# The chain in front of the state-space loop, by halves, and the first state's input made by VectorE

## The chip, the cores and the metric

One core of a Trainium2 chip runs the whole program. The metric is the device time of one launch in microseconds (us), the median of three runs. A 128 x 128 TensorE multiplies, VectorE (DVE) and ScalarE (ACT) work from SBUF and from PSUM, where TensorE writes, GpSimd (POOL) works from SBUF alone, and SyncE (SP) issues the DMAs. All five run their own instruction streams and wait for one another on semaphores.

## The reference, cut to what matters

Four sequences of 512 tokens with 128 features pass six layers: tree-routed feed-forward, attention, tree-routed feed-forward, mixture of experts, state-space block, mixture of experts. The change touches the state-space block:

```python
xz = rmsnorm(residual) @ W_in                     # 128 -> 2 x 256
x, z = split(xz)
x = silu(causal_conv4(x) + conv_b)
x_dbl = x @ W_x                                   # 64 + 16 + 16 columns
dt = softplus(x_dbl[:, :64] @ W_dt + b_dt)        # 256 channels
B, C = x_dbl[:, 64:80], x_dbl[:, 80:96]
# for each of 16 states n, over 512 tokens t:
#   h[t] = exp(dt[t] * A[:, n]) * h[t-1] + dt[t] * x[t] * B[t, n]
#   y[t] += h[t] * C[t, n]
out = residual + ((y + x * D) * silu(z)) @ W_out
```

softplus(v) is worked out as max(v, 0) + log(1 + u) with u = exp(-|v|); for small u the logarithm is corrected: with c = (1 + u) - 1, the result is max(v, 0) + u + min(max(log(1 + u) - c, -u*u/2), 0).

## The kernel before

Channels or tokens lie on the 128 partitions. The 24 units of work (6 layers, 2 sequences side by side, 2 pairs) run one after another; a unit's norm and transposes are done inside the unit before it, by `hand_over`, at fixed steps of its loop. Four units are state-space units, of which each does the following for one sequence, with its 256 channels as two halves m = 0, 1 of 128 partitions by 512 tokens.

**The front**, in the order of the chain. TensorE forms `W_in` products; ACT and DVE the convolution and silu, which give `n_xc`. TensorE multiplies by `W_x` (L1754): rows 0 to 63 of bank 4 are the input of dt, rows 64 to 95 are B and C. ACT copies the dt rows (L1003). TensorE makes B once more with tokens on partitions (L1758, 16 small matmuls to bank 5) and then the dt product of both halves (L1763, banks 0 and 1). ACT takes |v| for each half (L1006), then for both halves together u = exp(-|v|) (L1008), log(1 + u) (L1010), u*u/2 (L1011), and max(v, 0) by halves (L1013). DVE makes c (L1402), the difference (L1404), the two bounds and + u (L1406, L1407) over both halves at once, then dt (L1410) and dt*x (L1413) by halves. TensorE turns dt*x so that tokens lie on partitions (`dtx_rows`, L1461, banks 4 and 5).

**The loop** has 16 states with two halves each, numbered i = 0 to 31. ACT multiplies the turned dt*x by B per token (`inputs`, L1038, 4 instructions a state, tile `n_sx`) and makes exp(dt*A) (`decays`, L1030, tile `n_da`); TensorE turns the product back into PSUM (`drive(i)`, banks 0, 1 and 6 in turn, L1461); DVE scans (L1419, tile `n_h`); POOL multiplies by C (L791, `n_hc`), and TensorE adds that up with an identity matmul (L1784). C has to stand on all partitions, so SP writes its 16 rows to DRAM and reads them back broadcast, two states a DMA, into the ring `n_cs` of three (`state_rows`, L588 and L594). `n_sx[:, 0]` and `n_sx[:, 1]` also hold max(v, 0) and the correction ahead of the loop, `n_da` the logarithm and the square, and `n_h` |v| and u.

The order on each engine is the order of the code. DVE's `step` makes the instruction behind it wait until the one in it is done.

## Time and profile before

| | |
|---|---|
| median of 3 runs | 1404.59 us (1404.09 to 1405.96) |
| the profiled execution's own time | 1403.94 us |
| its span, first to last instruction | 1402.2 us |
| outside its span | 1.74 us |
| mean granted TensorE clock | 0.953 of 2.4 GHz |
| busy: PE, DVE, ACT, POOL | 1225.4, 916.9, 650.7, 237.3 us |
| state-space units | 4 of 24; first scans at 480.8, 565.0, 1169.3 and 1253.6 us |

Busy times overlap across engines, and a busy PE is not PE at its peak. In rows of the timeline the first number is the start in the span, the second the duration (of all merged instructions where there is a count over 1), and a bracket gives the idle time of the engine just before and what ended it.

### The profile page before, as it was taken

What the parts mean: (1) busy time and instruction counts of PE and PEld (TensorE: products, weight loads), DVE (VectorE), ACT (ScalarE), POOL (GpSimd) and SP (SyncE); (2) the same over time, 40 slices, a digit from 0 to 9 for tenths busy, and PEclk for the clock granted to TensorE, in tenths of its full rate; (3) what the DMA queues carried; (4) which work ended last, traced back from release to release, by engine and by line L of the source; (5) the groups of instructions that cost most, each with busy time, mean ns of one, the idle gap of its engine ahead of it and who ended that gap; (6) DMA issues with size and microseconds to landing.
All of it is one profiled execution on the core that took longest, in us unless ns stands there. A gap on an engine that the chain in (4) does not pass through costs nothing.

```text
span 1402.2 us, 17312 instructions
## 1 busy us (share of the span) xinstructions
PE 1225.4 (87%) x6135; PEld 798.9 (57%) x6184; DVE 916.9 (65%) x1802; ACT 650.7 (46%) x1199; POOL 237.3 (17%) x207
## 2 busy tenths in 40 slices
PE   5998788999899686889999967889999995969898
PEld 3676344577666343546667743446766653545565
DVE  6766766455567595877764766655555858859665
ACT  4543445443322785942234434453442247679122
POOL 3000000000020271741000010000002004718110
PEclk9999899999999798899999999999999996979999
DMA  6203020000110111120200122100010101112120
GB/s 216 61 23 105 25 69 19 2 0 1 61 60 1 58 64 46 61 76 1 69 23 0 38 69 78 33 2 1 1 40 21 61 22 55 46 46 76 61 68 8
DMA packets 31941, 62.02 MB, mean 44 GB/s; under 512 B 4112, under 2 KB 19760, under 8 KB 31664
## 3 DMA queue, kind: packets, MB, share of 16 engines
q1 hardware_dynamic: 31856, 60.93, 13.7%
q8 instruction: 49, 0.80, 0.2%
q14 instruction: 36, 0.29, 0.1%
HBM read 53.11 MB, written 8.32 MB: 44 GB/s over the span
## 4 chain that ended last, share of the span: by engine, by line
PE 66%; DVE 16%; ACT 8%; issue 3%; DMA 3%; POOL 2%; SPq 1%; another core or an unknown queue 0%; DVEq 0%; ACTq 0%; POOLq 0%
PE bank L1452 12%; PE bank L1454 12%; PE bank L1453 12%; PE bank L1618 8%; PE bank L1461 5%; DVE a_mx L1366 3%; DVE n_h L1419 3%; ACT n_sx L1038 3%; PE bank L1530 2%; PE bank L1784 2%; PE bank L1677 2%; PE bank L1591 2%; ACT n_da L1030 2%; DMA a_k<-stack_dram 2%; POOL n_hc L791 1%
## 5 line engine op out<-in xcount | busy, mean ns | idle before, releaser
L1215 DVE SCALAR_TENSOR_TENSOR f_hl<-bank,f_hh 128x512 fp32r<-128x512 f32 x192 | 131.8, 689 | 128.2 <-ACT f_hh L867 127.3
L867 ACT ACTIVATE f_hh<-bank 128x512 fp32r<-128x512 f32 x192 | 114.6, 597 | 188.2 <-PE bank L1530 150.0
L929 ACT ACTIVATE m_sl<-bank 128x512 f32<-128x512 f32 x144 | 85.8, 597 | 220.8 <-PE bank L1454 220.3
L791 POOL TENSOR_TENSOR n_hc<-n_h,n_cs 128x512 f32<-128x512 f32 x128 | 159.9, 1276 | 141.5 <-DVE n_h L1419 140.3
L1452 PE MATMUL bank<-xT_h,mw_h 128*128 128x512 f32 x288 | 160.8, 558 | 7.0 <-DVEq L514 4.3
L1419 DVE TENSOR_TENSOR_SCAN n_h<-n_da,bank 128x512 f32<-128x512 f32 x128 | 149.1, 1206 | 21.4 <-PE bank L1461 18.1
L1618 PE MATMUL bank<-m_h,mw 128*128 128x512 f32 x288 | 145.6, 594 | 0.0
L1366 DVE TENSOR_REDUCE a_mx<-bank 128x1 f32<-128x384 f32 (+3 forms) x176 | 106.1, 637 | 51.9 <-PE bank L1717 49.6
L1282 DVE TENSOR_TENSOR m_t<-m_sl,bank 128x512 f32<-128x512 f32 x128 | 87.9, 687 | 73.5 <-PE bank L1454 72.2
L1784 PE MATMUL bank<-n_hc,ident 128*128 128x512 f32 x256 | 132.4, 607 | 1.3 <-POOL n_hc L791 1.3
L947 ACT ACTIVATE a_p<-bank 128x1024 f32<-128x1024 f32 (+3 forms) x128 | 87.8, 703 | 91.1 <-PE bank L1654 90.0
L722 POOL TENSOR_TENSOR small<-small,half 128x4 f32<-128x4 f32 x24 | 24.3, 1011 | 597.1 <-DVE small L1117 596.7
L1461 PEld LDWEIGHTS bank<-ident,n_sx 128*128 128x128 f32 x512 | 67.3, 154 | 91.0 <-issue 68.0
L1454 PE MATMUL bank<-xT_h,mw_l 128*128 128x512 f32 x288 | 115.1, 400 | 0.0
L1452 PE MATMUL bank<-f_hh,fw_h 128*128 128x512 f32 x192 | 109.4, 570 | 6.1 <-DVE f_hl L1215 6.1
L1453 PE MATMUL bank<-xT_l,mw_h 128*128 128x512 f32 x288 | 114.6, 398 | 0.0
L1038 ACT ACTIVATE n_sx<-bank,n_bT 128x256 f32<-128x256 f32 x256 | 103.0, 536 | 9.7 <-PE bank L1461 9.7
L1461 PE MATMUL bank<-ident,n_sx 128*128 128x128 f32 x512 | 85.1, 299 | 25.4 <-DVE n_h L1419 14.5
L1030 ACT ACTIVATE n_da<-n_dt,amat 128x512 f32<-128x512 f32 x128 | 91.1, 794 | 17.7 <-DVE n_h L1419 12.9
L1715 PE MATMUL bank<-a_k,a_q 128*128 128x128 bf16 (+3 forms) x246 | 67.5, 317 | 29.5 <-DVE a_mx L1366 17.7
L1452 PE MATMUL bank<-xT_h,fw_h 128*128 128x512 f32 x192 | 83.2, 433 | 0.9 <-POOL b1w L705 0.9
L1290 DVE TENSOR_TENSOR m_h<-m_t,m_c 128x512 f32<-128x512 f32 x112 | 77.6, 693 | 4.4 <-DMA m_c<-comb_dram 0.7
(232 smaller groups left out, 2358.5 us busy)
## 6 DMA issues: line engine op xcount, KB each, us to landing
n_cs<-c_dram SPq DMA_DIRECT2D x32, 512.0 KB, 3.7
m_c<-comb_dram SPq DMA_DIRECT2D x28, 512.0 KB, 5.2
a_q<-stack_dram SPq DMA_DIRECT2D x8, 512.0 KB, 4.3
a_k<-stack_dram SPq DMA_DIRECT2D x16, 256.0 KB, 5.2
stage_fw<-in_fw_dram SPq DMA_DIRECT2D x6, 512.0 KB, 6.8
...
```

The costliest lines, as they stand in the source:

```text
L791: n_hcs.by(nc.gpsimd.tensor_tensor(n_hc[:, i % 4, :], n_h[:, i % 4, :], n_cs[:, j % C_RING, i // 2 % 2, :], ALU.mult))
L1030: n_das.by(act.activation(n_da[:, i % 4, :], n_dt[:, i % 2, :], ACT.Exp, scale=amat[:, i % 2, i // 2:i // 2 + 1]))
L1038: ins = act.activation(n_sx[:, n % 2, c, :], dtx_rows(c), ACT.Copy, scale=n_bT[:, c, n:n + 1])
L1215: f_lo.by(V.scalar_tensor_tensor(f_h[1][:, i % 4, :], bank[:, i % 3, :], 0.0, f_h[0][:, i % 4, :].bitcast(F32), ALU.max, ALU.subtract))
L1366: a_m1.by(V.tensor_reduce(a_mx[:, quad, qt, h0:h0 + nh], src, AX_X, ALU.max, negate=True))
L1419: n_scan.by(V.tensor_tensor_scan(n_h[:, i % 4, :], n_da[:, i % 4, :], drive(i), 0.0, ALU.mult, ALU.add))
L1452: mm(dst, w[0], x[0], start=start, stop=False)
L1453: mm(dst, w[0], x[1], start=False, stop=False)
L1454: return mm(dst, w[1], x[0], start=False, stop=stop)
L1461: ins = nc.tensor.transpose(dst(t), src(t), idn)
L1618: m_s2.by(mm(bank[:, 6, :], mw2[:, e, m, :], m_h[:, i2 % 3, :], start=i2 == 0, stop=i2 == MSTEPS - 1))
L1784: n_ya.by(mm(bank[:, 2 + m, :], ident[:], n_hc[:, i % 4, :], start=n == 2, stop=n == NSTATE + 1))
```

## The change

The dt product of both halves is put before the 16 matmuls of B on TensorE. max(v, 0) passes from ACT to DVE. The logarithm and the square are taken by halves, alternating; DVE adds u to max(v, 0) early, and the difference, the bounds, dt and dt*x go through for half 0 and then for half 1. dt is now one instruction that takes the last bound and adds. For state 0, DVE multiplies dt*x by B itself and writes the product straight to `drive(0)` and `drive(1)` in PSUM; the B row comes broadcast from DRAM (`n_brow`, in the third slot of the C ring), so the DMA to DRAM carries 32 rows in place of 16, and the third C load waits until that row has been read. ACT's `inputs(0)` and the eight transposes of state 0 are gone.

```diff
+        n_brow = n_cs[:, 2, 0, :]
...
-                n_cwr.by(sp.dma_start(c_dram, n_crow[80:96]))
+                n_cwr.by(sp.dma_start(c_dram, n_crow[64:96]))
                 sp.wait_ge(n_cwr.sem, n_cwr.at(k, 0))
+                n_b0.by(sp.dma_start(n_brow, c_dram[0:1].to_broadcast([P, T])))
                 for j in range(C_LOADS):
+                    if j == 2:
+
+                        sp.wait_ge(n_db0.sem, n_db0.at(k, 1))
...
-                n_lns.by(act.activation(n_ln, n_u, ACT.Ln, bias=1.0))
-                n_sqs.by(act.activation(n_sq, n_u, ACT.Square, scale=HALF_ROOT))
                 for m in range(2):
-                    n_poss.by(act.activation(n_pos[:, m, :], bank[:, m, :], ACT.Relu, bias=b_dt[:, m:m + 1]))
+                    n_lns.by(act.activation(n_ln[:, m], n_u[:, m], ACT.Ln, bias=1.0))
+                    n_sqs.by(act.activation(n_sq[:, m], n_u[:, m], ACT.Square, scale=HALF_ROOT))
...
-                inputs(k, 0)
...
+                for m in range(2):
+                    dve.wait_ge(n_abss.sem, n_abss.at(k, m))
+                    n_poss.by(V.tensor_scalar(n_pos[:, m], bank[:, m, :], b_dt[:, m:m + 1], 0.0, ALU.add, ALU.max))
                 dve.wait_ge(n_btp.sem, n_btp.at(k, 0))
                 n_bts.by(V.tensor_copy(flat(n_bT[:]), bank[:, 5, 0:NT * NSTATE]))
...
+                step(V.tensor_scalar(n_cor, n_u, 1.0, -1.0, ALU.add, ALU.add))
+                step(V.tensor_tensor(n_pos, n_pos, n_u, ALU.add))
...
+                for m in range(2):
+                    dve.wait_ge(n_lns.sem, n_lns.at(k, m))
+                    step(V.tensor_tensor(n_cor[:, m], n_ln[:, m], n_cor[:, m], ALU.subtract))
+                    dve.wait_ge(n_sqs.sem, n_sqs.at(k, m))
+                    step(V.scalar_tensor_tensor(n_cor[:, m], n_sq[:, m], -1.0, n_cor[:, m], ALU.mult, ALU.max))
+                    n_dts.by(V.scalar_tensor_tensor(n_dt[:, m], n_cor[:, m], 0.0, n_pos[:, m], ALU.min, ALU.add))
                     dve.wait_ge(n_dts.sem, n_dts.at(k, m))
                     n_dtxs.by(V.tensor_tensor(n_dtx[:, m], n_dt[:, m], n_xc[:, m], ALU.mult))
+                dve.wait_ge(n_b0.sem, n_b0.at(k, 0))
+                for m in range(2):
+                    dve.wait_ge(n_dtxs.sem, n_dtxs.at(k, m))
+                    n_db0.by(V.tensor_tensor(drive(m), n_dtx[:, m], n_brow, ALU.mult))
...
-                    if n < NSTATE:
-                        pe.wait_ge(n_sxs.sem, n_sxs.at(k, n))
+                    if 1 <= n < NSTATE:
+                        pe.wait_ge(n_sxs.sem, n_sxs.at(k, n - 1))
```

On DVE, in the first state-space unit, between the copy of B and C out of PSUM and the first two scans (a scan is printed as SCALAR_TENSOR_TENSOR here), the order before is this; `n_sx` is the correction and `n_xp` is dt*x:

```order
L1395 COPY n_hc<-bank 32x512
L1397 COPY n_bT<-bank 128x64
L1402 TENSOR_SCALAR n_sx<-n_h 128x1024
L1404 TENSOR_TENSOR n_sx<-n_da,n_sx 128x1024
L1406 SCALAR_TENSOR_TENSOR n_sx<-n_da,n_sx 128x1024
L1407 SCALAR_TENSOR_TENSOR n_sx<-n_sx,n_h 128x1024
L1410 TENSOR_TENSOR n_dt<-n_sx 128x512 x2
L1413 TENSOR_TENSOR n_xp<-n_dt,n_xc 128x512 x2
L1419 SCALAR_TENSOR_TENSOR n_h<-n_da,bank 128x512 x2
```

The order of the change, from the instruction that makes c on, after the two max(v, 0) (L1403) and the copy of B (L1405):

```order
L1409 TENSOR_SCALAR n_sx<-n_h 128x1024
L1410 TENSOR_TENSOR n_sx<-n_sx,n_h 128x1024
L1414 TENSOR_TENSOR n_sx<-n_da,n_sx 128x512
L1416 SCALAR_TENSOR_TENSOR n_sx<-n_da,n_sx 128x512
L1417 SCALAR_TENSOR_TENSOR n_dt<-n_sx 128x512
L1419 TENSOR_TENSOR n_xp<-n_dt,n_xc 128x512
L1414 TENSOR_TENSOR n_sx<-n_da,n_sx 128x512
L1416 SCALAR_TENSOR_TENSOR n_sx<-n_da,n_sx 128x512
L1417 SCALAR_TENSOR_TENSOR n_dt<-n_sx 128x512
L1419 TENSOR_TENSOR n_xp<-n_dt,n_xc 128x512
L1423 TENSOR_TENSOR bank<-n_xp,n_cs 128x512 x2
L1432 SCALAR_TENSOR_TENSOR n_h<-n_da,bank 128x512 x2
```

Four instructions over 1024 elements became two over 1024 and eight over 512, and two products that write PSUM (L1423) now stand straight before the scans.

On ACT the same place runs from the table load of the logarithm to the second state's decays; before:

```order
L1010 ACT_TABLE_LOAD
L1010 ACTIVATE n_da<-n_h 128x1024
L1011 ACTIVATE n_da<-n_h 128x1024
L1013 ACTIVATE n_sx<-bank,col 128x512 x2
L1030 ACT_TABLE_LOAD
L1030 ACTIVATE n_da<-n_dt,amat 128x512 x2
L1038 ACTIVATE n_sx<-bank,n_bT 128x256 x8
```

and in the change:

```order
L1018 ACT_TABLE_LOAD
L1018 ACTIVATE n_da<-n_h 128x512
L1019 ACTIVATE n_da<-n_h 128x512
L1018 ACTIVATE n_da<-n_h 128x512
L1019 ACTIVATE n_da<-n_h 128x512
L1035 ACT_TABLE_LOAD
L1035 ACTIVATE n_da<-n_dt,amat 128x512 x2
L1043 ACTIVATE n_sx<-bank,n_bT 128x256 x4
```

The number of table loads is the same, max(v, 0) is gone from ACT, and four `n_sx` instructions stand in place of eight.

On TensorE, from the `W_x` product on; before:

```order
L1754 MATMUL bank<-n_xc,wx 96x512 x2
L1758 MATMUL bank<-wx,n_xc 128x16 x8
L1763 MATMUL bank<-n_hc,wdt 128x512 x2
L1461 MATMUL bank<-ident,n_xp 128x128 x8
L1461 MATMUL bank<-ident,n_sx 128x128 x20
L1784 MATMUL bank<-n_hc,ident 128x512
```

and in the change:

```order
L1767 MATMUL bank<-n_xc,wx 96x512 x2
L1771 MATMUL bank<-n_hc,wdt 128x512 x2
L1774 MATMUL bank<-wx,n_xc 128x16 x8
L1474 MATMUL bank<-ident,n_xp 128x128 x8
L1474 MATMUL bank<-ident,n_sx 128x128 x12
L1796 MATMUL bank<-n_hc,ident 128x512
```

The dt product (L1763, now L1771) stands ahead of the B matmuls, and 12 transposes of `n_sx` in place of 20 come before the first addition of a state to y.

## Rows read from the trace of the kernel before

**Rows 1.** Timeline of the first unit's front: matmuls and ACT

```profile
461.98 1.85 PE L1758 MATMUL bank<-wx,n_xc 128*128 128x16 f32 x16
462.42 0.57 ACT L1003 ACTIVATE n_hc<-bank 64x512 f32<-64x512 f32 x1
...
463.77 2.10 PE L1763 MATMUL bank<-n_hc,wdt 64*128 64x512 f32 x4
...
466.62 1.06 ACT L1008 ACTIVATE n_h<-n_h 128x1024 f32<-128x1024 f32 x1
467.69 1.28 ACT L1010 ACT_TABLE_LOAD   x1
```

**Rows 2.** Timeline of the first unit's front: logarithm to loop

```profile
467.71 0.69 DVE L1402 TENSOR_SCALAR n_sx<-n_h 128x1024 f32<-128x1024 f32 x1 [3.61 <-ACT n_h L1008]
468.99 1.06 ACT L1010 ACTIVATE n_da<-n_h 128x1024 f32<-128x1024 f32 x1
469.95 1.04 ACT L1011 ACTIVATE n_da<-n_h 128x1024 f32<-128x1024 f32 x1
470.14 1.23 DVE L1404 TENSOR_TENSOR n_sx<-n_da,n_sx 128x1024 f32<-128x1024 f32 x1 [1.74 <-ACT n_da L1010]
...
472.16 1.28 ACT L1030 ACT_TABLE_LOAD   x1
...
473.92 1.29 DVE L1410 TENSOR_TENSOR n_dt<-n_sx 128x512 f32<-128x512 f32 x2
474.65 1.33 ACT L1030 ACTIVATE n_da<-n_dt,amat 128x512 f32<-128x512 f32 x2 [1.20 <-DVE n_dt L1410]
475.13 1.28 DVE L1413 TENSOR_TENSOR n_xp<-n_dt,n_xc 128x512 f32<-128x512 f32 x2
...
475.96 1.94 PE L1461 MATMUL bank<-ident,n_xp 128*128 128x128 f32 x8 [10.10 <-DVE n_xp L1413]
477.94 3.02 ACT L1038 ACTIVATE n_sx<-bank,n_bT 128x256 f32<-128x256 f32 x8 [1.96 <-PE bank L1461]
...
479.65 3.35 PE L1461 MATMUL bank<-ident,n_sx 128*128 128x128 f32 x16 [1.75 <-ACT n_sx L1038]
480.77 2.33 DVE L1419 TENSOR_TENSOR_SCAN n_h<-n_da,bank 128x512 f32<-128x512 f32 x2 [4.36 <-PE bank L1461]
480.80 1.38 ACT L1030 ACTIVATE n_da<-n_dt,amat 128x512 f32<-128x512 f32 x2
482.03 1.61 ACT L1038 ACTIVATE n_sx<-bank,n_bT 128x256 f32<-128x256 f32 x4
```

**Rows 3.** Timeline of DVE: third scan here, first scans of the last unit

```profile
484.52 4.54 DVE L1419 TENSOR_TENSOR_SCAN n_h<-n_da,bank 128x512 f32<-128x512 f32 x4
...
1253.60 2.33 DVE L1419 TENSOR_TENSOR_SCAN n_h<-n_da,bank 128x512 f32<-128x512 f32 x2 [4.36 <-PE bank L1461]
```

**Rows 4.** Timeline of ACT in the loop: its waits, units one and two

```profile
495.45 0.72 ACT L1030 ACTIVATE n_da<-n_dt,amat 128x512 f32<-128x512 f32 x1 [3.73 <-DVE n_h L1419]
...
576.95 0.72 ACT L1030 ACTIVATE n_da<-n_dt,amat 128x512 f32<-128x512 f32 x1 [0.97 <-DVE n_h L1419]
578.06 0.73 ACT L1030 ACTIVATE n_da<-n_dt,amat 128x512 f32<-128x512 f32 x1 [0.39 <-DVE n_h L1419]
```

**Rows 5.** Durations of one line: times min/median/max in ns, then form

```profile
L996 ACT ACTIVATE n_xc<-n_hc x4: 629/630/630, 458.0 to 1231.4; 128x512 f32<-128x512 f32 x4
L1397 DVE COPY n_bT<-bank x4: 224/224/225, 463.9 to 1236.8; 128x64 f32<-128x64 f32 x4
L1383 DVE TENSOR_SCALAR n_hc<-n_xp,col x4: 545/546/548, 455.1 to 1228.5; 128x512 f32<-128x512 f32 x4
```

**Rows 6.** Timeline of SP: the C loads of the first unit

```profile
464.55 24.10 SPq L594 DMA_DIRECT2D n_cs<-c_dram  x4
```

**Rows 7.** Windows: busy by engine, granted clock, DMA share, GB/s

```profile
470.00:472.00 2.00, 0.00 (x0) 0.00 (x0) 1.82 (x2) 2.00 (x4) 0.00 (x0) 0.50 0.15 61
482.00:484.00 2.00, 1.31 (x10) 1.00 (x9) 1.97 (x6) 2.00 (x6) 1.93 (x2) 0.86 0.00 0
```

More of the change, by code:

```diff
@@ L469, in program @@
         n_us = sig("n_us", "mamba", 1)
-        n_lns = sig("n_lns", "mamba", 1)
-        n_sqs = sig("n_sqs", "mamba", 1)
+        n_lns = sig("n_lns", "mamba", 2)
+        n_sqs = sig("n_sqs", "mamba", 2)
         n_poss = sig("n_poss", "mamba", 2)
+        n_b0 = sig("n_b0", "mamba", 1, 16)
+        n_db0 = sig("n_db0", "mamba", 2)
         n_dts = sig("n_dts", "mamba", 2)
@@ L475, in program @@
         n_dxt = sig("n_dxt", "mamba", 1)
-        n_sxs = sig("n_sxs", "mamba", NSTATE)
+        n_sxs = sig("n_sxs", "mamba", NSTATE - 1)
         n_das = sig("n_das", "mamba", 2 * NSTATE)
-        n_dbs = sig("n_dbs", "mamba", 2 * NSTATE)
+        n_dbs = sig("n_dbs", "mamba", 2 * NSTATE - 2)
         n_scan = sig("n_scan", "mamba", 2 * NSTATE)
@@ L1033, in inputs @@
             def inputs(k, n):
-                if n >= 2:
-                    act.wait_ge(n_dbs.sem, n_dbs.at(k, 2 * n - 3))
+                if n >= 3:
+                    act.wait_ge(n_dbs.sem, n_dbs.at(k, 2 * n - 5))
                 for c in range(NT):
@@ L1400, in mamba @@
                 dve.wait_ge(n_us.sem, n_us.at(k, 0))
+                dve.wait_ge(n_poss.sem, n_poss.at(k, 1))
+                step(V.tensor_scalar(n_cor, n_u, 1.0, -1.0, ALU.add, ALU.add))
+                step(V.tensor_tensor(n_pos, n_pos, n_u, ALU.add))
                 dve.wait_ge(n_sil.sem, n_sil.at(k, 3))
-                step(V.tensor_scalar(n_cor, n_u, 1.0, -1.0, ALU.add, ALU.add))
-                dve.wait_ge(n_lns.sem, n_lns.at(k, 0))
-                step(V.tensor_tensor(n_cor, n_ln, n_cor, ALU.subtract))
-                dve.wait_ge(n_sqs.sem, n_sqs.at(k, 0))
-                step(V.scalar_tensor_tensor(n_cor, n_sq, -1.0, n_cor, ALU.mult, ALU.max))
-                step(V.scalar_tensor_tensor(n_cor, n_cor, 0.0, n_u, ALU.min, ALU.add))
-                for m in range(NHALF):
-                    dve.wait_ge(n_poss.sem, n_poss.at(k, m))
-                    n_dts.by(V.tensor_tensor(n_dt[:, m], n_cor[:, m], n_pos[:, m], ALU.add))
-                for m in range(NHALF):
+                for m in range(2):
[4 more added lines that the diff above has]
+                    n_dts.by(V.scalar_tensor_tensor(n_dt[:, m], n_cor[:, m], 0.0, n_pos[:, m], ALU.min, ALU.add))
                     dve.wait_ge(n_dts.sem, n_dts.at(k, m))
                     n_dtxs.by(V.tensor_tensor(n_dtx[:, m], n_dt[:, m], n_xc[:, m], ALU.mult))
+                dve.wait_ge(n_b0.sem, n_b0.at(k, 0))
+                for m in range(2):
+                    dve.wait_ge(n_dtxs.sem, n_dtxs.at(k, m))
+                    n_db0.by(V.tensor_tensor(drive(m), n_dtx[:, m], n_brow, ALU.mult))
                 for i in range(2 * NSTATE):
-                    dve.wait_ge(n_dbs.sem, n_dbs.at(k, i))
+                    if i < 2:
+                        dve.wait_ge(n_db0.sem, n_db0.at(k, i))
+                    else:
+                        dve.wait_ge(n_dbs.sem, n_dbs.at(k, i - 2))
                     dve.wait_ge(n_das.sem, n_das.at(k, i))
@@ L1755, in mamba @@
                 n_xdb.by(ins)
+                pe.wait_ge(n_dtc.sem, n_dtc.at(k, 0))
+                for m in range(2):
+                    n_dtp.by(mm(bank[:, m, :], wdt[:, m, :], n_dtr, start=True, stop=True))
                 for c in range(NT):
@@ L1760, in mamba @@
                 n_btp.by(ins)
-                pe.wait_ge(n_dtc.sem, n_dtc.at(k, 0))
-                for m in range(2):
-                    n_dtp.by(mm(bank[:, m, :], wdt[:, m, :], n_dtr, start=True, stop=True))
                 pe.wait_ge(n_bts.sem, n_bts.at(k, 0))
```

4 lines of the change are left out of this document (2 added, 2 removed).

## The prediction

> **What bounds the kernel now.** The page comes first: TensorE is the busiest engine, but that is a mean over 24 units, and the change lies in four stretches of some 18 us each, the fronts of the state-space units. So I read the timeline there. From the dt product to the first scan it shows one thread that passes from engine to engine, never two of them busy with what the end waits for. TensorE multiplies B for 1.85 us and then dt; ACT has had the input of dt ready since 462.42 + 0.57 = 462.99, but the dt product starts at 463.77, because the B matmuls stand ahead of it [rows 1]. Then u ends at 467.68, a table load and the logarithm end at 470.05, and only there does DVE begin three instructions of 1.22 to 1.23 us over both halves, two for dt and two for dt*x [rows 2]. TensorE idles 10.10 us, turns dt*x in 1.94 us, ACT multiplies by B, TensorE turns back, and DVE, which was done at 476.41, scans at 480.77 after 4.36 us of idleness [rows 2]. All four units repeat this: the last unit's first scan waits the same 4.36 us [rows 3].
>
> Whether time won there reaches the end is read from the loop. After two scans and some 1.4 us of statistics DVE scans again at 484.52 [rows 3]; through the middle of the loop the timeline shows it busy without a gap, while ACT waits for scans: 3.73 us in the first unit, 0.97 and 0.39 us in the second [rows 4]. So DVE's start sets the loop up to there. From there to the end ACT and TensorE share the bound, and both hang on that same moment. A loop that starts d earlier thus ends d earlier, as long as ACT isn't left behind by more than those waits.
>
> **The change part by part**, with the first unit's times. Dependent DVE instructions start their duration plus 0.03 us apart (three from 470.14 to 473.92, 1.26 each [rows 2]), independent ones of 512 elements 0.61 us apart (two in 1.29, each of them 0.68 to 0.69).
>
> *dt before B.* The dt product can start 0.06 us after 462.99, so at 463.05 in place of 463.77. Everything on ACT up to u comes 0.72 us earlier; u ends at 466.96. The B matmuls move behind it: 463.05 + 2.10 + 1.85 = 467.00, then DVE's copy of 0.22 us [rows 5] ends at 467.29. It was hidden before; now it stands before the instruction that makes c, and costs that 0.3 us.
>
> *Early part on DVE.* c takes 0.69 us as before [rows 2], 467.32 to 468.01; max(v, 0) + u costs like a two-source instruction over 1024, 1.23 us, and ends at 469.27. It is 1.23 us moved to where DVE used to wait for the logarithm (1.74 us of idleness). The two max(v, 0) on DVE lie between |v| and u, where DVE had nothing (3.61 us idle). Their duration isn't in the trace for this form; between 0.55 (512 elements from SBUF, [rows 5]) and 0.75 they are done by 466.7, so the price is nil.
>
> *Logarithm by halves.* Table load of 1.28 us, then 0.63 us for 512 elements on ACT [rows 5], 0.10 less from start to start: 468.27 to 468.90 for the first logarithm, the last square done by 470.5. DVE is ready at 469.30, so ACT no longer sets the pace; 0.4 us of its lead is unused. No table load is added.
>
> *The chain by halves.* Half 0: difference, bound, dt at 0.72 us each (0.69 for 512 elements) from 469.30, dt*x at 471.46. Half 1 starts 0.61 us later at 472.07, and its dt*x runs 474.23 to 474.91. The last dt*x ended at 476.41 before, so 1.5 us are won. ACT's table load for the exponential ends at 471.8, decays run at once behind dt of each half, and the second is done by 474.9, before any scan needs it.
>
> *State 0 by DVE.* Two products of 512 elements. No DVE instruction of this trace writes PSUM; the bounds are 0.55 us (the fastest of 512 elements [rows 5]) and 1.17 us (half of two scans in 2.33 [rows 2]). I take 0.69, what two SBUF sources cost here, since the arithmetic is the same. Starts at 474.84 and 475.44, first scan at 476.05. Before: 480.77. **Won: 4.72 us.** The way over TensorE and ACT (1.94 + 1.5 + 1.1 us) is no longer in front of the scans.
>
> *What is late next.* dt*x of half 1 is done at 474.91, its four transposes take half of 1.94 us, so ACT starts `inputs(1)` at 475.97, 1.61 us long; it is ready for state 1's decays at 477.4 against 480.80, a lead of 3.4 us [rows 2]. State 1 is turned from 477.6 on in 1.1 us (479.65 to 480.77 before), ready at 478.7; the third scan wants it at 484.52 - 4.72 = 479.80. State 2 follows: ACT 478.6 to 480.2, turned by 481.35, wanted at 482.1. The first scans are fed. ACT's lead is 1.3 us short of DVE's, which the waits of 3.73 us, and of 0.97 + 0.39 = 1.36 us in the second unit, just take up [rows 4].
>
> *DMAs.* SP issues its loads from 464.55, when the write to DRAM has landed [rows 6]. Three loads of 512 KB were through early in the 470 to 472 window (share 0.15 [rows 7]). Now the 256 KB of the B row go first and two loads behind: at most five sixths of that, so before 470.3, and the row is wanted at 474.84. The write has 32 rows in place of 16; it lies between the end of the `W_x` product, near 462, and 464.55, so twice as long would cost the row 2.5 us at most of its 4.5 us of margin. The third load leaves at 476.1 with nothing behind it but loads that wait for POOL anyway; POOL wants it from the ninth scan, after 489.
>
> *TensorE's clock.* It stands at 0.50 through the front and is back at full speed in the window 482 to 484 (0.86, [rows 7]), some 3 us after the transposes of 479.65 began. In the new order the fifth state-half's transposes and the first addition to y fall at 480.3 to 483. At 1.2 GHz that addition takes an estimated 1.5 to 2 us (two of the four dt instructions of 2.10 us at full speed, doubled at most), and the sixth scan slips by 0.6 to 0.9 us; at 2.4 GHz it doesn't. I take 0.2 us. The Trainium skill says ("TensorE: Matmul & The Clock Gate", What's actually happening) that the clock is half by default and sustained activity releases it; the trace agrees, 0.50 and then 0.86. By that rule TensorE, which now has eight transposes fewer and more pauses between short bursts, would come back later, if at all earlier; that is a rival below.
>
> *Sum.* 4.72 - 0.2 = 4.5 us a unit, 18.0 us in four. The profiled execution took 1403.94 us (span 1402.2 and 1.74 around it); 1403.94 - 18.0 = 1385.9. The median is 0.65 us above that execution, so 1386.6 us.
>
> **The rivals.**
>
> *The loop keeps ACT's lead only.* If ACT or TensorE binds in the first states, the gain is ACT's 3.4 us a unit: 1404.6 - 13.6 = 1391.0. For it: ACT has no gap for the first 10 us of the loop, and the second unit's slack exceeds the need by 0.06 us. Against it: the waits of [rows 4].
>
> *The clock comes back late.* Then the sixth scan slips 0.9 us, and further transposes with it, say 2 us a unit: 1404.6 - 4 x 2.7 = 1393.8. The clock decides from how soon dense work begins, which is 2 us earlier than before.
>
> *The time is already covered, or the B row is late.* If the row landed at 479.6 the first scan would stand where it stood: 1404.6. Against it the margin of 4.5 us.
>
> *Slower.* TensorE falls to 1.2 GHz within the last 15 us of the loop, where it binds. There a state-half takes TensorE an estimated 1.3 us at full speed: half of the dt product's 2.10 us [rows 1], and four transposes, which take a quarter of 1.94 us at 2.4 GHz [rows 2], less some overlap. At half speed that is about 1.3 us more, and with four such state-halves a unit 5.2 us are lost against 4.7 won: 1404.6 + 4 x 0.5 = 1406.6, and from 3.6 state-halves on it decides. For it: the clock also falls inside the loop in some units, after pauses. Against it: in that stretch TensorE has no pauses.
>
> **How the numbers follow.** Forecast 0.64 (1384 to 1389), ACT's lead 0.14, late clock 0.10, covered 0.04, slower 0.04, and 0.04 for more than forecast. The low end: PSUM writes of 0.55 us and no slip give 5.0 us, 1384.6; with 0.1 us less on each of the four shared steps 1383. The high end: PSUM writes of 1.17 us cost 0.96 more and the sixth scan 0.6, leaving 3.2 us, 1392; with the late clock 1393.8. Range 1383 to 1393.5. A measurement of this kernel can tell about 0.2% (2.8 us) from no change: faster than that 0.91, within it 0.05, slower 0.04.
>
> **What would show it.** In the changed profile: the dt product starts right after ACT's copy; DVE's chain from the first difference to the first scan is 6.7 us without a gap; two DVE products into `bank` of about 0.69 us each; the first scans without idle time before them; from first scan to the end of each loop 51.6 us as before or 0.2 more. It is wrong if that last distance grows by 1 us or more (ACT or the clock), if those products take over a microsecond, or if DVE waits on the DMA of the B row.

## The result, and the profile after

The change takes 1390.65 us (median of 4 runs, 1390.03 to 1391.93) against 1404.34 us for the kernel before (4 runs, 1402.42 to 1405.96) in the same comparison: ratio 0.9904, 95% interval 0.9887 to 0.9921. It is 13.7 us faster, where 18.0 were forecast. The profiled span is 1388.2 us in place of 1402.2.

The page after: busy time, share of the span and instructions of each engine, and TensorE's granted clock in 40 slices.

```profile
PE 1234.8 (89%) x6152; PEld 800.1 (58%) x6152; DVE 927.7 (67%) x1826; ACT 641.8 (46%) x1183; POOL 237.6 (17%) x207
...
PEclk9999899999999798899999999999999996979899
```

TensorE is busy for 9.4 us more, with 32 transposes fewer: some of its work ran at a lower clock. To see where, each unit is cut in two at places that stand in both programs. The **front** runs from the start of DVE's copy of B and C (L1395, now L1400) to the first scan, the **loop** from there to the first `n_da<-n_xc,col,bank` on DVE (L1428, now L1441).

| us, units 1 to 4 | fronts | loops | sum |
|---|---|---|---|
| before | 18.52, 18.47, 18.41, 18.48 | 51.60, 51.51, 51.59, 51.52 | 280.10 |
| after | 14.37, 13.67, 14.76, 14.28 | 52.10, 52.19, 52.29, 52.34 | 266.00 |
| won | 4.15, 4.80, 3.65, 4.20 | -0.50, -0.68, -0.70, -0.82 | 14.1 |

The fronts won 16.8 us, the loops lost 2.7, and the difference of 14.1 is the result within 0.4 us.

**The front** of unit 1, timeline of the changed kernel; this answers to [rows 1, 2]:

```profile
462.16 0.57 ACT L1010 ACTIVATE n_hc<-bank 64x512 f32<-64x512 f32 x1
462.79 1.98 PE L1771 MATMUL bank<-n_hc,wdt 64*128 64x512 f32 x4 [0.90 <-ACT n_hc L1010]
...
464.70 2.74 PE L1774 MATMUL bank<-wx,n_xc 128*128 128x16 f32 x16
...
465.53 1.06 ACT L1015 ACTIVATE n_h<-n_h 128x1024 f32<-128x1024 f32 x1
...
467.48 0.22 DVE L1405 COPY n_bT<-bank 128x64 f32<-128x64 f32 x1 [1.20 <-PE bank L1774]
467.62 0.68 DVE L1409 TENSOR_SCALAR n_sx<-n_h 128x1024 f32<-128x1024 f32 x1
...
469.60 0.69 DVE L1414 TENSOR_TENSOR n_sx<-n_da,n_sx 128x512 f32<-128x512 f32 x1
...
474.56 0.69 DVE L1419 TENSOR_TENSOR n_xp<-n_dt,n_xc 128x512 f32<-128x512 f32 x1
...
475.17 1.29 DVE L1423 TENSOR_TENSOR bank<-n_xp,n_cs 128x512 f32<-128x512 f32 x2
...
476.37 2.32 DVE L1432 TENSOR_TENSOR_SCAN n_h<-n_da,bank 128x512 f32<-128x512 f32 x2
```

The dt product starts 0.06 us behind ACT's copy, the first scan has no bracket, and from the first difference to the scan DVE takes 476.37 - 469.60 = 6.77 us without a gap. One row is off: u is ready at 465.53 + 1.06 = 466.59, yet c (L1409) starts at 467.62, because DVE's copy of B stands ahead of it and waits for TensorE. The B matmuls took 2.74 us where 1.85 had been measured [rows 1]. In the four units they take 2.74, 1.96, 3.13 and 2.58 us, and the fronts follow: 14.37, 13.67, 14.76 and 14.28.

**The loop.** TensorE and DVE in its first 10 us, timeline after:

```profile
478.17 1.94 PE L1474 MATMUL bank<-ident,n_sx 128*128 128x128 f32 x8 [1.75 <-ACT n_sx L1043]
...
480.10 3.43 DVE L1432 TENSOR_TENSOR_SCAN n_h<-n_da,bank 128x512 f32<-128x512 f32 x3
...
481.66 1.91 PE L1796 MATMUL bank<-n_hc,ident 128*128 128x512 f32 x2
...
483.37 1.06 PE L1474 MATMUL bank<-ident,n_sx 128*128 128x128 f32 x4
...
484.47 1.22 DVE L1432 TENSOR_TENSOR_SCAN n_h<-n_da,bank 128x512 f32<-128x512 f32 x1 [0.93 <-PE bank L1474]
```

The first addition to y takes 1.91 us, the transposes behind it 1.06, and the sixth scan waits 0.93 us for them. It does so in all four units, at 8.10 us from the first scan. The clock over that stretch, windows after (columns as in [rows 7]):

```profile
466.00:468.00 2.00, 1.44 (x7) 1.33 (x7) 0.80 (x3) 1.97 (x3) 0.00 (x0) 0.50 0.46 168
...
482.00:484.00 2.00, 2.00 (x5) 0.86 (x4) 1.53 (x2) 2.00 (x6) 2.00 (x3) 0.50 0.00 0
484.00:486.00 2.00, 2.00 (x6) 0.86 (x5) 1.47 (x4) 2.00 (x6) 1.11 (x1) 0.50 0.52 172
486.00:488.00 2.00, 2.00 (x12) 1.44 (x11) 1.93 (x5) 1.30 (x4) 1.27 (x1) 0.96 0.28 90
```

The clock is at 0.50, 1.2 GHz, until 486, nearly 10 us into the loop. In the other units it comes back 8 to 10 us into it. Before, the loop's first scan was at 480.77 and the full clock back some 2 us later: 0.86 in 482 to 484 [rows 7].

### The profile page after: what moved, and what is told of

Read it like the earlier page. It is cut to its first block, busy times and chain, and to the rows that moved or that the text cites. A ratio compares the mean times of both kernels' runs of the same rounds, so it can differ in the third digit from the quotient of the medians.

```text
span 1388.2 us, 17313 instructions
## 1 busy us (share of the span) xinstructions
PE 1234.8 (89%) x6152; PEld 800.1 (58%) x6152; DVE 927.7 (67%) x1826; ACT 641.8 (46%) x1183; POOL 237.6 (17%) x207
## 3 DMA queue, kind: packets, MB, share of 16 engines
q1 hardware_dynamic: 32496, 62.11, 14.1%
## 4 chain that ended last, share of the span: by engine, by line
PE 69%; DVE 16%; ACT 6%; issue 3%; DMA 3%; POOL 2%; SPq 2%; DVEq 0%; ACTq 0%; POOLq 0%
PE bank L1465 12%; PE bank L1466 12%; PE bank L1467 12%; PE bank L1631 9%; PE bank L1474 6%; PE bank L1796 4%; DVE a_mx L1371 3%; PE bank L1543 3%; PE bank L1604 2%; PE bank L1690 2%; ACT n_sx L1043 2%; DVE n_h L1432 2%; PE bank L1665 1%; DMA a_k<-stack_dram 1%; PE bank L1728 1%
## 5 line engine op out<-in xcount | busy, mean ns | idle before, releaser
L1796 PE MATMUL bank<-n_hc,ident 128*128 128x512 f32 x256 | 136.9, 625 | 1.5 <-POOL n_hc L798 1.5
L1474 PEld LDWEIGHTS bank<-ident,n_sx 128*128 128x128 f32 x480 | 63.6, 154 | 83.5 <-issue 61.8
L1728 PE MATMUL bank<-a_k,a_q 128*128 128x128 bf16 (+3 forms) x256 | 72.4, 324 | 32.3 <-DVE a_mx L1371 20.4
L1043 ACT ACTIVATE n_sx<-bank,n_bT 128x256 f32<-128x256 f32 x240 | 97.5, 541 | 7.1 <-PE bank L1474 7.1
L1474 PE MATMUL bank<-ident,n_sx 128*128 128x128 f32 x480 | 81.2, 299 | 17.0 <-ACT n_sx L1043 10.8
L1465 PEld LDWEIGHTS bank<-xT_h,mw_h 128*128 128x128 f32 x288 | 55.6, 193 | 43.5 <-issue 27.8
```

The source lines that it names most:

```text
L1043: ins = act.activation(n_sx[:, n % 2, c, :], dtx_rows(c), ACT.Copy, scale=n_bT[:, c, n:n + 1])
L1465: mm(dst, w[0], x[0], start=start, stop=False)
L1474: ins = nc.tensor.transpose(dst(t), src(t), idn)
L1796: n_ya.by(mm(bank[:, 2 + m, :], ident[:], n_hc[:, i % 4, :], start=n == 2, stop=n == NSTATE + 1))
```

## The experiments

The theory after this reading: (F) the fronts are as forecast, but for the copy of B, which waits for matmuls at half clock; (L) the loops are longer because TensorE is at half clock for the first 8 to 10 us of them. The scans say where: in the change the seventh scan starts 0.47 to 0.67 us later after the first than before, in every unit, and unit 4 loses another 0.35 between the 12th and the 15th; hardly anything is lost elsewhere. The rivals: ACT's lead is what limits the gain (it gives the measured 1391 too), and the halves, not state 0, carry the gain or the loss.

All edits are against the changed kernel, e11 against the one before. The kernels before had medians of 1404.7 (e1 to e4), 1405.3 (e5 to e8), 1407.0 (e9 to e11) and 1405.7 us (e12), and runs of one kernel scattered by some 0.3%, so the fronts and loops of the profiles say more than the medians:

| | median us | ratio (95%) | fronts | loops | sum |
|---|---|---|---|---|---|
| the change | 1390.65 | 0.9904 (0.9887 to 0.9921) | 13.7 to 14.8 | 52.1 to 52.3 | 266.0 |
| e1 B first | 1390.99 | 0.9905 (0.9881 to 0.9930) | 14.2 | 52.1 to 52.2 | 265.4 |
| e2 copy late | 1386.86 | 0.9868 (0.9843 to 0.9892) | 13.5 to 13.6 | 52.0 to 52.1 | 262.6 |
| e3 y late | 1394.38 | 0.9926 (0.9904 to 0.9948) | 13.6 to 14.9 | 52.1 to 52.9 | 267.4 |
| e4 warm | 1385.99 | 0.9864 (0.9840 to 0.9887) | 13.6 to 14.5 | 51.6 to 51.9 | 262.7 |
| e5 state 0 by ACT | 1400.02 | 0.9955 (0.9937 to 0.9974) | 16.6 to 17.7 | 51.5 to 51.6 | 274.9 |
| e6 whole | 1388.89 | 0.9879 (0.9855 to 0.9903) | 13.2 to 14.2 | 52.5 to 52.9 | 265.7 |
| e7 copy late, y late | 1388.78 | 0.9874 (0.9849 to 0.9898) | 13.5 to 13.6 | 52.0 to 52.4 | 262.8 |
| e8 whole, copy late, warm | 1388.12 | 0.9870 (0.9847 to 0.9894) | 13.2 to 13.3 | 51.7 to 52.5 | 261.4 |
| e9 copy late, warm | 1385.78 | 0.9845 (0.9826 to 0.9863) | 13.5 to 13.6 | 52.0 to 52.8 | 263.8 |
| e10 as e8, fewer extras | 1385.97 | 0.9845 (0.9825 to 0.9866) | 13.2 to 13.3 | 51.5 to 52.3 | 260.5 |
| e11 before, only state 0 by DVE | 1398.98 | 0.9941 (0.9924 to 0.9959) | 15.2 | 52.4 to 52.7 | 271.0 |
| e12 as e9, warmed earlier | 1388.04 | 0.9871 (0.9852 to 0.9891) | 13.5 to 13.6 | 51.5 to 52.8 | 261.8 |

### The copy of B: e1 and e2

e1 puts the B matmuls back ahead of the dt product. e2 keeps dt first and moves DVE's copy of B behind max(v, 0) + u:

```diff
-                pe.wait_ge(n_dtc.sem, n_dtc.at(k, 0))
-                for m in range(2):
-                    n_dtp.by(mm(bank[:, m, :], wdt[:, m, :], n_dtr, start=True, stop=True))
                 ... the 16 matmuls of B
+                pe.wait_ge(n_dtc.sem, n_dtc.at(k, 0))
+                for m in range(2):
+                    n_dtp.by(mm(bank[:, m, :], wdt[:, m, :], n_dtr, start=True, stop=True))
```

> The changed kernel with the 16 B matmuls put back ahead of the dt product. My theory (the B matmuls behind dt run into TensorE's fall to 1.2 GHz and hold the copy of B, and with it DVE): u comes 0.72 us later, but the copy of B is out of the way, so from the copy of B and C to the first scan all four units take 14.2 us, against 14.37, 13.67, 14.76 and 14.28 in the changed kernel; total within 0.5 us of it. Rival (moving dt ahead is worth its 0.72 us a unit): 2.9 us slower than the changed kernel, that is 1393.5 us.

```diff
-                dve.wait_ge(n_btp.sem, n_btp.at(k, 0))
-                n_bts.by(V.tensor_copy(flat(n_bT[:]), bank[:, 5, 0:NT * NSTATE]))
...
                 step(V.tensor_tensor(n_pos, n_pos, n_u, ALU.add))
+                dve.wait_ge(n_btp.sem, n_btp.at(k, 0))
+                n_bts.by(V.tensor_copy(flat(n_bT[:]), bank[:, 5, 0:NT * NSTATE]))
```

> The changed kernel with DVE's copy of B behind the addition of u to max(v, 0). My theory: c starts 0.03 us after u, and the first scan comes 13.6 us after the copy of B and C in all units, 0.05 to 1.1 us earlier than now, 2.6 us over four units: 1388.0 us. Rival (the front is not what sets the loop's end, ACT's lead is): no change, 1390.6 us.

e1: fronts of 14.15 to 14.23, in sum 0.3 us less than the change's, as its text expected: with the copy where it stood, dt first had won nothing. e2: fronts of 13.51 to 13.58, all four alike, with DVE in unit 1 as follows (timeline of e2):

```profile
466.83 0.69 DVE L1407 TENSOR_SCALAR n_sx<-n_h 128x1024 f32<-128x1024 f32 x1 [0.34 <-ACT n_h L1015]
467.55 1.23 DVE L1408 TENSOR_TENSOR n_sx<-n_sx,n_h 128x1024 f32<-128x1024 f32 x1
468.81 0.23 DVE L1410 COPY n_bT<-bank 128x64 f32<-128x64 f32 x1
...
475.72 2.32 DVE L1432 TENSOR_TENSOR_SCAN n_h<-n_da,bank 128x512 f32<-128x512 f32 x2
```

c now waits for u from ACT and the copy for nobody. The fronts are 54.2 us in sum in place of 57.1, and the ratio is 0.9868 in place of 0.9904. The B matmuls themselves are as uneven as before, 2.93, 1.96, 3.15 and 1.96 us; they only hold nobody up any more. Part F is shown. It also means that fronts of kernels which keep the copy where it was differ by up to 1.3 us (e3) with the moment at which the clock falls, whatever their edit.

### The wait at the sixth scan: e3 and e7

e3 adds to y one state-half later, so that the transposes of the sixth scan pass ahead of the first additions; e7 has e2's edit too and moves only the first addition.

```diff
-                for i in range(2 * NSTATE + 4):
+                for i in range(2 * NSTATE + 5):
...
-                    if i >= 4:
-                        pe.wait_ge(n_hcs.sem, n_hcs.at(k, i - 4))
+                    if i >= 5:
+                        j = i - 5
+                        pe.wait_ge(n_hcs.sem, n_hcs.at(k, j))
...
```

> The changed kernel with TensorE's additions to y one step later in the loop. My theory (the sixth scan waits 0.93 us because the first addition at 1.2 GHz stands ahead of its transposes): the wait of 0.93 us is gone, the loop takes 51.5 to 51.7 us from first scan to the end against 52.1 to 52.3, 2.0 to 2.8 us over four units: 1388 to 1388.6 us. Rival (the loop keeps ACT's lead only): the wait moves elsewhere and the time stays at 1390.6 us.

```diff
-                    if i >= 4:
-                        pe.wait_ge(n_hcs.sem, n_hcs.at(k, i - 4))
...
+                    for j in ([] if i < 5 else [0, 1] if i == 5 else [i - 4]):
+                        pe.wait_ge(n_hcs.sem, n_hcs.at(k, j))
...
```

> The changed kernel with the copy of B later on DVE, and with only the first addition to y moved, behind the transposes of the sixth state-half; from there on the order is as before, so the end of the loop has no extra addition. My theory (the wait of 0.93 us is a TensorE queue at 1.2 GHz, and a lag at the end ate what the later additions won): the fronts take 13.5 us, the sixth scan doesn't wait, and the loops take 51.5 to 51.8 us: about 4 us less than the changed kernel, 1386.5 us. Rival (the loop's length comes from elsewhere, as DVE's small instructions beside POOL): fronts 13.5 us, loops 52.1 us, 1388 us.

The wait is gone in both, and the loops aren't shorter: 52.1 to 52.9 and 52.0 to 52.4, where at most 51.8 were expected; e3's median of 1394.4 us is even above the change's. In units 1 and 3 of e3 the last addition comes later as well (from the start of the 31st scan to the end of the loop 5.67 us in place of 4.81). So taking the 0.93 us wait away doesn't give its time back. What DVE does behind the sixth scan shows the reason, and it is the rival that e7's text names. Timeline of DVE, first of the kernel before, where this stage starts at 488.99, then of the change:

```profile
488.99 0.57 DVE L1091 TENSOR_TENSOR small<-small 128x4 f32<-128x4 f32 x1
489.59 1.20 DVE L1092 TENSOR_TENSOR small<-small 128x4 f32<-128x4 f32 x1
...
491.23 1.11 DVE L1127 TENSOR_SCALAR xn<-X,mv,small 128x128 f32<-128x128 f32 x4
```

```profile
485.60 0.14 DVE L1096 TENSOR_TENSOR small<-small 128x4 f32<-128x4 f32 x1
485.77 0.16 DVE L1097 TENSOR_TENSOR small<-small 128x4 f32<-128x4 f32 x1
...
486.37 2.03 DVE L1132 TENSOR_SCALAR xn<-X,mv,small 128x128 f32<-128x128 f32 x4
```

The same small instructions take 0.57 and 1.20 us, or 0.14 and 0.16, and the four of 128 elements 1.11 or 2.03 us in sum. POOL's timeline there, before, then of the change:

```profile
485.81 4.97 POOL L791 TENSOR_TENSOR n_hc<-n_h,n_cs 128x512 f32<-128x512 f32 x4
```

```profile
483.84 1.27 POOL L798 TENSOR_TENSOR n_hc<-n_h,n_cs 128x512 f32<-128x512 f32 x1
486.28 1.27 POOL L798 TENSOR_TENSOR n_hc<-n_h,n_cs 128x512 f32<-128x512 f32 x1 [1.17 <-PE bank L1796]
```

Before, L1092 ends at 490.79, when POOL's fourth multiply ends (490.78). In the change L1096 and L1097 fall into POOL's pause from 485.11 to 486.28, and L1132 into the multiply that follows. Over all 14 traces, 129 instructions TENSOR_TENSOR of 4 elements on `small` start beside such a multiply, and each of them ends within 0.04 us of it; alone they take 0.16 us. The batch norm instructions (L1101 and L1104 before) aren't held: 448 of them start beside a multiply and take 0.15 and 0.28 us as elsewhere. The stage between two scans is 4.66 us long in the change (485.60 to 490.26) and 5.21 before, and gives back half of the wait.

In e7 the same stage goes the other way. DVE's timeline in its unit 1, then POOL's:

```profile
484.90 1.15 DVE L1097 TENSOR_TENSOR small<-small 128x4 f32<-128x4 f32 x1
...
486.29 1.14 DVE L1102 TENSOR_TENSOR small<-small 128x4 f32<-128x4 f32 x1
```

```profile
484.76 2.64 POOL L798 TENSOR_TENSOR n_hc<-n_h,n_cs 128x512 f32<-128x512 f32 x2 [0.71 <-PE bank L1796]
```

POOL waited 0.71 us for the first addition to y, which frees its buffer, and its two multiplies then catch one small instruction each; the stage takes 5.69 us (484.74 to 490.43). In all four units of e7 two small instructions are caught, and the seventh scan starts 0.47 to 0.53 us later after the first than before, though no scan up to there waits. So TensorE's slow start reaches DVE by two ways: through the transposes that a scan wants, and through the additions that POOL's buffers want. Moving the additions swaps the one for the other. Unit 1 of e7 loses 0.3 us more at the 15th and 17th scans, where the clock is at 0.50 again.

### TensorE's clock: e4

Twelve matmul instructions of 512 columns stand behind the B matmuls and four behind each half's transposes of dt*x (one call of `mm` here makes two instructions, so the text below counts ten). They go to a PSUM bank that is free there, and nothing reads them.

```diff
+                for _ in range(6):
+                    mm(bank[:, 2, :], ident[:], n_xc[:, 0, :], start=True, stop=True)
...
-                n_dxt.by(ins)
+                    if m == 1:
+                        n_dxt.by(ins)
+                    for _ in range((2, 2)[m]):
+                        mm(bank[:, 2, :], ident[:], n_xc[:, 0, :], start=True, stop=True)
```

> The changed kernel with ten extra matmuls a state-space unit into a PSUM bank that is free there (no output uses them), six behind the B matmuls and two behind each half's transposes. Clock theory: the granted clock stays at 1.0 through the front, the sixth scan doesn't wait, and the loops take 51.6 us: 2.0 to 3 us faster than the changed kernel, 1388 us. Rival (ACT's lead): the clock stays up and the time doesn't move. If the extra matmuls stand in the way of the transposes, the first scan isn't later but ACT's inputs are, and the time rises.

Windows of e4 (columns as before), and TensorE's timeline there:

```profile
474.00:476.00 2.00, 2.00 (x9) 1.15 (x8) 1.93 (x4) 0.72 (x1) 0.00 (x0) 1.00 0.00 0
...
482.00:484.00 2.00, 1.57 (x8) 1.05 (x9) 1.72 (x2) 2.00 (x6) 2.00 (x2) 1.00 0.00 0
```

```profile
467.62 7.88 PE L1778 MATMUL bank<-n_xc,ident 128*128 128x512 f32 x12
475.34 0.60 PE L1474 MATMUL bank<-ident,n_xp 128*128 128x128 f32 x4
...
482.92 1.02 PE L1801 MATMUL bank<-n_hc,ident 128*128 128x512 f32 x2
483.78 0.60 PE L1474 MATMUL bank<-ident,n_sx 128*128 128x128 f32 x4
```

The clock is at 1.00 all through the first part of the loop, in all four units, four transposes take 0.60 us in place of 1.06, the addition 1.02 in place of 1.91, and the loops are 51.91, 51.91, 51.61 and 51.76: 1.7 of the 2.7 us lost in the loops come back. ACT's instructions and their order are those of the change, and it starts later: its third exp(dt*A) begins 1.93 to 2.86 us behind the first scan, where it begins 1.53 behind it in the change and 0.03 before. A limit by ACT's lead would have grown; the loops got shorter. Part L holds for those 1.7 us.

Of the other 1.0 us, 0.3 is a wait at the fifth scan of unit 1, and 0.6 is ACT's lead after all: the 13th scans of units 2 and 4 wait 0.43 and 0.28 us for transposes that wait for ACT (section on e12 below). The extra matmuls between the two halves had held ACT back.

### Which part of the change carries the gain: e5, e6, e11

e5 is the change without its last part: state 0 goes over ACT and TensorE again.

```diff
+                inputs(k, 0)
...
-                dve.wait_ge(n_b0.sem, n_b0.at(k, 0))
-                for m in range(2):
-                    dve.wait_ge(n_dtxs.sem, n_dtxs.at(k, m))
-                    n_db0.by(V.tensor_tensor(drive(m), n_dtx[:, m], n_brow, ALU.mult))
```

> The changed kernel with state 0 made by ACT and TensorE again and no B row from DRAM. My theory (the products on DVE take the way over TensorE, ACT and TensorE out of the path): from dt*x of half 1 to the first scan 4.36 us as in the kernel before, in place of 1.12; the front takes 3.2 us longer in each unit, near 17.5 us, the sixth scan no longer waits, loops 51.5 to 51.7 us: 10.5 us over four units, 1401 us. Rival (the loop was bound by ACT and TensorE, so the early scans bought little): the front grows by 3.2 us and the loops shrink by more than 1.5 us each, total under 1397 us.

e11 is the kernel before with that last part alone (the edits to `n_brow`, `c_dram`, `n_b0` and `n_db0` of the diff ahead of the prediction, with ACT's `inputs(0)` and the transposes of state 0 taken out, and no other).

> The kernel before with one part of the change alone: state 0 by DVE from the B row; order, logarithm and max(v, 0) as before. My theory: from the last dt*x to the first scan 1.12 in place of 4.36 us, fronts of 15.3 us; dt*x comes for both halves back to back, so ACT and TensorE follow late as in e6_whole and the loops take 52.5 to 52.9 us: 12.9 us won in the fronts, 4 to 5 lost in the loops, 8 to 9 us less than before: about 1396 us. Rival (the DVE products only pay together with the halves): under 4 us gained.

e5 wins 5.2 us in fronts and loops (the first scans wait 4.04 us for TensorE), e11 9.1; together 14.3, against 14.1 for the change: the two parts add up. In e11 the fronts win 3.2 to 3.3 us each and the loops lose 0.8 to 1.2, with the sixth scan's wait at 1.24 to 1.25 us. In e5 the loops are as before, 51.5 to 51.6. So the loops' loss belongs to state 0 by DVE, which lets the scans start when TensorE has done only eight transposes since the front.

e6 takes the logarithm, the square, the difference and the bound over both halves at once again and keeps all else.

```diff
-                for m in range(2):
-                    n_lns.by(act.activation(n_ln[:, m], n_u[:, m], ACT.Ln, bias=1.0))
-                    n_sqs.by(act.activation(n_sq[:, m], n_u[:, m], ACT.Square, scale=HALF_ROOT))
+                n_lns.by(act.activation(n_ln, n_u, ACT.Ln, bias=1.0))
+                n_sqs.by(act.activation(n_sq, n_u, ACT.Square, scale=HALF_ROOT))
...
+                step(V.tensor_tensor(n_cor, n_ln, n_cor, ALU.subtract))
+                step(V.scalar_tensor_tensor(n_cor, n_sq, -1.0, n_cor, ALU.mult, ALU.max))
```

> The changed kernel with logarithm, square, difference and bound over both halves in one instruction each; the fused dt stays, by halves. My theory (DVE sets the pace of this chain, so halves only add four starts of an instruction): from the difference to the end of the last dt*x 5.05 us in place of 5.65, the front 0.6 us shorter in each unit (13.8, 13.1, 14.2, 13.7), total 2.4 us less, 1388.2 us. Rival (halves overlap ACT's logarithm with DVE): DVE waits for the whole logarithm and square, the front gets 0.5 us longer or more, total above 1392 us.

Timeline of DVE in e6:

```profile
469.98 1.23 DVE L1412 TENSOR_TENSOR n_sx<-n_da,n_sx 128x1024 f32<-128x1024 f32 x1
...
476.12 2.32 DVE L1432 TENSOR_TENSOR_SCAN n_h<-n_da,bank 128x512 f32<-128x512 f32 x2
...
484.53 1.22 DVE L1432 TENSOR_TENSOR_SCAN n_h<-n_da,bank 128x512 f32<-128x512 f32 x1 [1.24 <-PE bank L1474]
```

From the difference to the first scan it takes 6.14 us in place of 6.77: fewer and longer instructions, with fewer starts between them, are quicker once DVE sets the pace. But both halves' transposes then come together at the end, and the sixth scan waits 1.24 us in place of 0.93; the loops are 52.5 to 52.9. The sum, 265.7, is that of the change, though the fronts also hold B matmuls of other lengths (3.16, 2.59, 1.96 and 2.58 us). By the chain alone whole instructions win 0.63 us a unit, 2.5 in four, and the loops lose 2.1. In the change the halves win next to nothing: of the 1.5 us that the prediction gave to "the chain by halves", none is due to the halving itself, but to the instructions saved and moved.

### Together: e8, e9, e10 and e12

e8 is e6 with the late copy and e4's matmuls; e9 is e2 with e4's matmuls; e10 is e8 with 14 extra matmul instructions behind B and none between the halves (`range(7)`, `range((0, 2)[m])`); e12 is e9 with two of them ahead of the dt product, ten behind B, and two instead of four behind the second half.

> The changed kernel with the later copy of B, with logarithm to bound over both halves at once, and with the ten extra matmuls that keep TensorE's clock up. If the three add: fronts of 13.0 to 13.1 us, loops of 51.6 to 51.9 us, 5.3 us less than the changed kernel for the fronts and 2 us for the loops, 1383.5 us. If ACT's lead binds: the fronts shrink and the loops grow by the same, and the time stays near 1387 us.

> The changed kernel with the later copy of B and the ten extra matmuls, halves kept. My theory (two separate losses: the copy of B behind slow B matmuls in the front, TensorE at 1.2 GHz in the first states): fronts 13.5 to 13.6 us and loops 51.6 to 51.9 us in all units, together 261.4 us over the four units against 266.0 now and 262.6 with the later copy alone: 4.6 us less than the changed kernel, 1386 us. Rival (one loss, seen twice): no better than the later copy alone, 1387 us, with loops back at 52.1.

> As e8_best, but with no extra matmul between the transposes of the two halves of dt*x, where two of them held the second half's back (7 behind the B matmuls, none between, 2 behind). My theory: fronts 13.2 us, ACT starts 1.7 us earlier than there, loops 51.6 to 51.9 us in all four units, 260 us together, 6 us less than the changed kernel: 1384.7 us. Rival (with both halves at once ACT gets dt*x too late after the first scan whatever TensorE does): loops of 52.3 us or more in two or four units, no better than e9_copy_warm.

> The later copy of B, halves kept, and nine extra matmuls placed otherwise: one where TensorE waits 0.90 us for ACT ahead of the dt product, five behind the B matmuls, two and one behind the transposes of the halves. Theory: in the first and third unit of e9_copy_warm the clock fell already in the B matmuls, and the extra ones, at 1.2 GHz, then stood in front of the transposes of dt*x; with no idle time ahead of dt the clock stays at 1.0 in all units, and fronts of 13.5 to 13.6 us go with loops of 51.6 to 52.0 us in all four, 261.5 us together against 263.8 there: 0.5 to 2.5 us less than it, near 1384.5 us where the kernel before takes 1405 us. Rival (the clock falls whatever TensorE does there): two units with loops above 52.5 us again.

The extra matmuls are work too. Timelines of e9, TensorE and then DVE:

```profile
466.18 7.41 PE L1778 MATMUL bank<-n_xc,ident 128*128 128x512 f32 x12
...
475.58 0.60 PE L1474 MATMUL bank<-ident,n_xp 128*128 128x128 f32 x4
...
478.59 2.33 DVE L1432 TENSOR_TENSOR_SCAN n_h<-n_da,bank 128x512 f32<-128x512 f32 x2 [0.92 <-PE bank L1474]
```

The second half's dt*x was there at 472.73, but its transposes stand behind the extra matmuls and start at 475.58 (0.05 us behind dt*x in the change), and the third scan waits 0.92 us. This happens in units 1 and 3, where the clock had fallen before the extras and they took 7.41 and 7.61 us; there the loops are 52.83, in the others 51.98. The sum is 263.8, where 261.4 were expected. e10, with none between the halves, has loops of 51.48 in units 2 and 4, as short as before, and 52.3 in 1 and 3, where the clock had fallen, the extras hold the transposes up and the third scan waits 0.39 us. Its rival named two such units, but by another cause, both halves at once, and units 2 and 4 show that these are no hindrance. e8 misses its 1383.5 us too: loops of 51.7 in units 1 and 3, and of 52.5 in 2 and 4, where the 13th scan waits 0.92 us.

In e12 the clock stays at 1.00 in unit 1 from the B matmuls, which take 1.96 us, until 13 us into the loop, the transposes of dt*x start as early as in the change, and the loop is 51.60. So it is in unit 3 (51.62), and unit 4 has 51.51. With the clock up and ACT not held back the loops are those of the kernel before, and nothing of the 0.5 to 0.8 us is left. Its forecast of four such loops fails in unit 2, with 52.83, and its median of 1388.0 us is 3.5 above the forecast.

Timeline and window of e12, first unit:

```profile
466.74 1.96 PE L1775 MATMUL bank<-wx,n_xc 128*128 128x16 f32 x16
```

```profile
468.00:470.00 2.00, 2.00 (x11) 1.28 (x11) 1.63 (x3) 1.97 (x3) 0.00 (x0) 1.00 0.63 175
```

Timeline of e12's unit 2 at the 13th scan, ACT, TensorE and DVE:

```profile
573.37 1.75 ACT L839 ACTIVATE xn<-X,small 128x128 f32<-128x128 f32 x4
...
574.91 1.67 ACT L1043 ACTIVATE n_sx<-bank,n_bT 128x256 f32<-128x256 f32 x4
...
576.63 0.66 PE L1474 MATMUL bank<-ident,n_sx 128*128 128x128 f32 x4 [0.81 <-ACT n_sx L1043]
...
577.33 2.52 DVE L1432 TENSOR_TENSOR_SCAN n_h<-n_da,bank 128x512 f32<-128x512 f32 x2 [0.94 <-PE bank L1474]
```

TensorE is at full clock there (1.00 from 572 to 578) and waits for ACT, which has just spent 1.75 us on the next unit's `xn` (`hand_over`). That is ACT's lead as a limit, and it stands in the second and fourth units, where this work lies. In unit 2 the clock had fallen ahead of the extras, which held the transposes up, and ACT's third exp(dt*A) began 2.99 us behind the first scan. The other kernels fit to one number, a slack of 1.6 us. Take as ACT's delay how much later than in the kernel before its third exp(dt*A) begins behind the first scan, here 2.99 - 0.03 = 2.96. The part of it above 1.6 us is what the unit had already lost by its seventh scan plus the wait at the 13th: 1.36 against 0.41 + 0.94 here, and within 0.05 us in units 2 and 4 of e4, e8 and e9. In the change ACT's delay is 1.50 us and stays just inside.

By ratio e9 and e10 are best (both 0.9845), 21 us below the kernel before of their chip. Their intervals overlap those of e2, e4, e6, e7, e8 and e12, so which of them is best isn't settled; e9's and e10's lie wholly below the change's own (0.9887 to 0.9921). e2 needs no extra matmuls and moves two lines.

## Why the prediction was right or wrong

**Right in direction and mechanism.** The first scan doesn't wait, state 0 by DVE carries most of the gain, and time won at the first scan reaches the end of the loop: 14.1 of 16.8 us. The rest was lost on the way. The measured median lies 4 us above the forecast of 1386.6, inside the range: 2.1 us of that are the fronts and 1.9 the loops.

- *State 0 by DVE*: right. The products into PSUM take what two SBUF sources cost here. Durations of that line in the change:

```profile
L1423 DVE TENSOR_TENSOR bank<-n_xp,n_cs x8: 690/692/694, 475.2 to 1236.6; 128x512 f32<-128x512 f32 x8
```

- *Early part on DVE*: right. The two max(v, 0) from PSUM take 1.61 us together, 0.75 each, the upper bound, and are done at 466.28, before u: the price is nil.
- *Logarithm by halves, the chain by halves*: the times are right to 0.02 us (6.77 from the first difference, 6.75 by the prediction's starts). The reason wasn't: e6 shows that the halves cost DVE 0.6 us against whole instructions, and give it back in the loop.
- *dt before B*: **the first term that failed.** The product did start right behind ACT's copy. But the prediction carried 1.85 us for the B matmuls over from the trace, where they ran right behind the `W_x` product. It also said that the clock stands at 0.50 through the front; the rows that it shows start at 470. At the B matmuls of the kernel before the clock was up, and it fell behind them (window before):

```profile
462.00:464.00 2.00, 2.00 (x18) 1.97 (x17) 0.81 (x2) 0.98 (x3) 0.00 (x0) 1.00 0.06 12
464.00:466.00 2.00, 1.86 (x4) 0.43 (x3) 0.10 (x1) 0.79 (x2) 0.00 (x0) 0.88 0.24 51
```

  Behind dt they run after a pause of 0.90 us and into the stretch in which the clock falls (0.92 in 464 to 466, then 0.50), and take 2.74, 1.96, 3.13 and 2.58 us. The copy cost some 1 us in unit 1 and not 0.3. In four fronts 16.8 us were won in place of 18.9 (4 x 4.72); e2 wins them, and 0.8 us more, by moving a copy of 0.22 us.
- *TensorE's clock*: **the second.** 0.2 us a unit was taken, and 0.6 to 0.9 named as the other end. The loops lost 0.50 to 0.82. The prediction leaned on the return before, some 3 us behind the start of the first transposes of `n_sx`; in the change these start at 478.17 and the clock is back at 486, 8 us behind it. The return came within one run of 16 transposes before [rows 2]; now TensorE has eight, a pause of 0.65 us, and from 480.75 on work without a pause, over 5 us of it at 0.50. The rule that was quoted, activity releases a clock that is half by default (the Trainium skill, "TensorE: Matmul & The Clock Gate", What's actually happening), pointed the right way: later. The trace agrees, 0.50 until 486; it was given 0.10 as a rival, with a price of 2 us a unit that is three times what was lost.
- *What is late next*: right that ACT's lead is enough, by 0.1 us. ACT won 2.90 us (third exp(dt*A) at 477.90 for 480.80) and not 3.4, DVE 4.40; the 1.50 between them were covered by a slack of 1.6 in units 2 and 4, which the prediction put at 1.36. The rival "the loop keeps ACT's lead only" gives 1391.0, the measured number, and that is chance: with the 2.90 it would give 1393.0. In the change DVE waits for TensorE at the sixth scan, and e4 shortens the loops with ACT later. It becomes true once the clock is up: in units 2 and 4 of e4, e8 and e9 and in unit 2 of e12 the 13th scan waits for ACT.
- *DMAs*: right. The B row is never waited for: the products start 0.61 us behind the last dt*x, as independent instructions do.
- Of "what would show it", the test on the loop (wrong if it grows by 1 us) was passed, but a growth of 0.5 to 0.8 in all four units is 2.7 us, a fifth of the gain.

**Open.** Why the clock falls at another moment in each unit, so that the B matmuls take 1.96 us in one and 3.13 in the next, no run here settles. An order in which the extra matmuls delay nothing in any unit wasn't found: e12 has three such units of four. That the small instructions cost e7 its 0.5 us is read from its traces and wasn't tested by an edit of its own.
